# Filter taps summed in four strips of the array with moving powers and then transposed; VectorE takes the norms' constants; products in two halves

## The chip, the cores and the metric

The kernel runs on one core of a Trainium2 chip. The metric is the device time of one execution in microseconds, and the median of several runs counts. TensorE multiplies matrices into PSUM, VectorE and ScalarE work elementwise on SBUF and PSUM, GpSimd works elementwise on SBUF alone, and SyncE issues the transfers.

## What is computed

The input is 16 batches of 256 tokens with 128 channels. Four residual layers follow each other, each on a layer norm of its input; everything before the first expert layer is the part that this case is about.

```python
x = L0_attn_a_u
x = x + _L0_attn_a_ref(_layernorm(x, axis=-1), ...)   # long convolution
x = x + _L0_ffn_ref(_layernorm(x, axis=-1), ...)      # 8 experts, the best 2 of each token
x = x + _L0_attn_b_ref(_layernorm(x, axis=-1), ...)   # causal attention, 16 heads, 4 query sets
x = x + _L0_ffn_ref(_layernorm(x, axis=-1), ...)

# in _L0_attn_a_ref: the filter K, and its product with the input in the frequency domain
at = dt[:, None, None] * A[None, None, :] * t[None, :, None]
K = jnp.einsum('mn,mln->ml', C_re, jnp.exp(at))
y = jnp.fft.irfft(u_f * k_f, n=2 * L_)[..., :L_]
return y.transpose(0, 2, 1) + u * D
```

## The kernel before

Each engine has a queue written out by hand; what stands in it runs in that order, and engines wait for each other by semaphores. The program has five stages: the taps of the filter, the convolution, the first experts, attention, the second experts. In the profile the taps and the convolution take the first 81 us.

**Taps.** The filter K of 256 taps for 128 channels is a sum over 64 states of decaying powers. `z` holds the decay rates. `grid` (L508) multiplies `z` by the tap numbers 0 to 63, ScalarE makes `powers` of it with Exp (L490), in five pieces of 8, 8, 16, 16 and 16 columns of `z` (`GRIDS`); VectorE makes four of the grids and GpSimd the fourth. `leap` holds the four leaps of 64 taps, and `weight` (L527) is leap times `C_re`. TensorE (L551) takes 32 groups of four channels: `powers` (128 columns) is the weight that is loaded, `weight` (16 columns) the operand that moves, and each group writes 128 x 16 values into bank 6. When all 32 are done (`tapped`), VectorE (L537) and ScalarE (L494) move halves of the bank into `ktap`, VectorE adds the skip weight `skip_d` to tap 0 (L542), and TensorE transforms `ktap` with `taps` (L561). ScalarE copies the result to `khat` (L498).

**Convolution.** The 16 batches go through in four chunks of four batches. For each chunk VectorE takes statistics (L384, L388), GpSimd adds epsilon to the variance (`vareps`, L361) and raises it to -1/2 (`rstd`, L363), and for chunks 1 to 3 it also makes `neg_mean` (L395) and `offset` (L398). ScalarE normalizes the chunk with them (L414); of chunk 0 VectorE does that itself (L404). Then the two halves of the sequence are folded (L420): VectorE takes the differences, GpSimd the sums, and both of chunk 0 are VectorE's. TensorE transforms the folded chunk into banks 0 to 3 (L620), VectorE multiplies these banks by `khat` in eight products (L631), GpSimd combines the products in four steps into `yhat` (L642, L644), TensorE transforms back in 16 matrix instructions (L654), and VectorE adds the result to `stream` (L662). TensorE's queue has the forward transform of chunk ch + 1 ahead of the inverse of chunk ch. GpSimd also cuts the low halves of the expert weights (L602) in between, from what ScalarE has scaled and rounded (L575, L577).

**Later stages.** Every later norm goes the same way in groups of four tiles: VectorE L352 and L356, GpSimd L361 and L363, VectorE L369. There are 24 of them: 8 each ahead of the first experts, attention and the second experts. In the expert stages VectorE also subtracts halves (L873) and accumulates (L916), GpSimd subtracts the other halves (L880), and TensorE works at L850 and L904.

## Time and profile before

| What | Value |
|---|---|
| Median of 3 runs | 842.37 us (841.85 to 843.05) |
| The profiled execution | 843.33 us |
| Its span in the trace | 841.6 us |
| TensorE busy in the span | 789.6 us, 94% |
| ScalarE busy | 707.8 us, 84% |
| VectorE busy | 658.0 us, 78% |
| GpSimd busy | 559.9 us, 67% |
| Chain that ended last | TensorE 64%, ScalarE 12%, VectorE 8%, GpSimd 5%, issue 9% |

All times within the trace count from the start of the span. The shares are means over stages with different limits, so a stage is read from its own rows: the chain of work in order of time says which engine each stretch waited for, and the timeline says what stood around it. A matrix product in 32-bit floats shows as two matrix instructions in the trace, a transpose as one.

### The profile page before, as it was taken

What the parts mean: (1) busy time and instruction counts of PE and PEld (TensorE: products, weight loads), DVE (VectorE), ACT (ScalarE), POOL (GpSimd) and SP (SyncE); (2) the same over time, 40 slices, a digit from 0 to 9 for tenths busy, and PEclk for the clock granted to TensorE, in tenths of its full rate; (3) what the DMA queues carried; (4) which work ended last, traced back from release to release, by engine and by line L of the source; (5) the groups of instructions that cost most, each with busy time, mean ns of one, the idle gap of its engine ahead of it and who ended that gap; (6) DMA issues with size and microseconds to landing.
All of it is one profiled execution on the core that took longest, in us unless ns stands there. A gap on an engine that the chain in (4) does not pass through costs nothing.

```text
span 841.6 us, 20311 instructions
## 1 busy us (share of the span) xinstructions
PE 789.6 (94%) x7689; PEld 437.8 (52%) x7689; DVE 658.0 (78%) x1925; ACT 707.8 (84%) x888; POOL 559.9 (67%) x631
## 2 busy tenths in 40 slices
PE   6699998899999899999999999999999999999995
PEld 6344676566677433333333333333333777777774
DVE  5686899999997566777777777777645999888884
ACT  4431897788889799999999999999998899999984
POOL 4694556455543688888888889888887554445442
PEclk9999999999999899999999999999999999999998
DMA  9201000000003323343333434433310000000000
GB/s 291 78 26 76 2 2 2 2 2 1 2 17 87 99 80 95 91 93 92 96 93 82 91 101 102 101 95 87 102 22 1 2 14 14 15 14 14 14 14 16
DMA packets 38521, 46.87 MB, mean 56 GB/s; under 512 B 6185, under 2 KB 23858, under 8 KB 38418
## 3 DMA queue, kind: packets, MB, share of 16 engines
q1 hardware_dynamic: 38418, 45.51, 20.7%
q8 instruction: 62, 1.02, 0.5%
q14 instruction: 41, 0.34, 0.1%
HBM read 28.71 MB, written 16.78 MB: 54 GB/s over the span
## 4 chain that ended last, share of the span: by engine, by line
PE 64%; ACT 12%; issue 9%; DVE 8%; POOL 5%; DMA 0%; ACTq 0%; POOLq 0%
PE psum L904 16%; PE psum L850 16%; PE psum L1202 12%; ACT prob L1160 11%; PE psum L1151 5%; PE psum L1260 4%; PE psum L654 4%; DVE mixed L916 3%; POOL prob L1175 2%; PE psum L551 2%; PE psum L1044 1%; PE psum L725 1%; PE psum L620 1%; DVE hidden_parts_first L873 1%; PE psum L700 1%
## 5 line engine op out<-in xcount | busy, mean ns | idle before, releaser
L1160 ACT ACTIVATE prob<-psum 128x1536 f32<-128x1536 f32 x256 | 347.8, 1498 | 17.4 <-PE psum L1151 17.4
L1202 PE MATMUL psum<-prob,vstack 128*32 128x256 f32 (+1 forms) x2048 | 207.3, 500 | 1.6 <-DVE o_tok L1210 1.6
L850 PE MATMUL psum<-xt_parts,w_parts 128*128 128x512 f16 x768 | 186.7, 379 | 2.7 <-POOL wqkv_parts L602 2.7
L916 DVE SCALAR_TENSOR_TENSOR mixed<-psum,comb_y,mixed 128x128 f32<-128x128 f32 x512 | 143.1, 339 | 2.1 <-PE psum L904 2.1
L880 POOL TENSOR_TENSOR hidden_parts_second<-hidden_second,hidden_parts_second 128x512 f16<-128x512 f32 x64 | 78.9, 1234 | 91.7 <-ACT hidden_parts_second L866 91.7
L880 POOL TENSOR_TENSOR hidden_parts_first<-hidden_first,hidden_parts_first 128x512 f16<-128x512 f32 x64 | 77.9, 1221 | 77.2 <-ACT hidden_parts_first L866 77.1
L864 ACT ACTIVATE hidden_first<-psum,b 128x512 f32<-128x512 f32 x128 | 88.4, 690 | 31.0 <-PE psum L850 23.9
L1170 POOL TENSOR_SCALAR_AFFINE_SELECT prob<-prob 128x512 f32<-128x512 f32 x128 | 82.5, 644 | 42.1 <-ACT prob L1160 36.5
L1151 PE MATMUL psum<-qstack,kstack 32*128 32x512 f16 x768 | 100.4, 387 | 9.1 <-POOL prob L1175 4.4
L1151 PEld LDWEIGHTS psum<-qstack,kstack 32*128 32x128 f16 x768 | 24.9, 91 | 159.0 <-ACT prob L1160 137.3
L850 PEld LDWEIGHTS psum<-xt_parts,w_parts 128*128 128x128 f16 x768 | 71.9, 99 | 67.2 <-POOL wqkv_parts L602 2.8
L864 ACT ACTIVATE hidden_second<-psum,b 128x512 f32<-128x512 f32 x128 | 88.3, 690 | 19.2 <-PE psum L850 15.5
L904 PE MATMUL psum<-w_parts,hidden_parts_first 128*128 128x128 f16 x1536 | 96.0, 219 | 8.3 <-issue 5.2
L904 PEld LDWEIGHTS psum<-w_parts,hidden_parts_first 128*128 128x128 f16 x1536 | 90.3, 98 | 25.1 <-issue 13.3
L904 PEld LDWEIGHTS psum<-w_parts,hidden_parts_second 128*128 128x128 f16 x1536 | 90.9, 98 | 16.4 <-issue 2.0
L904 PE MATMUL psum<-w_parts,hidden_parts_second 128*128 128x128 f16 x1536 | 96.0, 219 | 1.4 <-DVE mixed L916 1.0
L1210 DVE STREAM_TRANSPOSE o_tok<-psum 128x512 f32<-128x512 f32 x64 | 45.9, 717 | 56.8 <-PE psum L1202 56.7
L866 ACT ACTIVATE hidden_parts_first<-psum,b 128x512 f16<-128x512 f32 x128 | 88.4, 691 | 0.0
L866 ACT ACTIVATE hidden_parts_second<-psum,b 128x512 f16<-128x512 f32 x128 | 88.3, 690 | 0.0
L1175 POOL TENSOR_SCALAR_AFFINE_SELECT prob<-prob 128x1280 f32<-128x1280 f32 x64 | 85.1, 1330 | 4.6
L1172 POOL TENSOR_SCALAR_AFFINE_SELECT prob<-prob 128x512 f32<-128x512 f32 x128 | 82.5, 645 | 0.0
L1202 PEld LDWEIGHTS psum<-prob,vstack 128*32 128x32 f32 x2048 | 47.3, 109 | 53.7 <-issue 30.9
(133 smaller groups left out, 1050.8 us busy)
## 6 DMA issues: line engine op xcount, KB each, us to landing
qstack<-qk_parts SPq DMA_DIRECT2D x128, 128.0 KB, 3.5
qk_parts<-parts SPq DMA_DIRECT2D x64, 192.0 KB, 3.2
kstack<-qk_parts SPq DMA_DIRECT2D x128, 32.0 KB, 3.4
stream<-L_attn_a_u SPq DMA_DIRECT2D x4, 512.0 KB, 8.0
kept_x<-stream SPq DMA_DIRECT2D x4, 512.0 KB, 2.7
out<-mixed SPq DMA_DIRECT2D x8, 256.0 KB, 2.3
mirror<-u_mirror SPq DMA_DIRECT2D x4, 256.0 KB, 7.1
w_whole<-L_ffn_W SPq DMA_DIRECT2D x1, 1024.0 KB, 9.4
```

The lines of the kernel that those rows point to most:

```text
L850: last = e.matmul(bank(u % 4), m.w1[:, w_part, ex, cols], xt_parts[:, s, x_part, :], start=(n == 0), stop=(n == len(PRODUCTS) - 1))
L864: last = e.activation(m.hidden[:, r, k, :], bank(u % 4), ACT.Relu, scale=scale, bias=bias)
L866: last = e.activation(m.hidden_parts[:, r, 0, k, :], bank(u % 4), ACT.Relu, scale=scale, bias=bias)
L880: e.tensor_tensor(m.hidden_parts[:, r, 1, 1, :], m.hidden[:, r, 1, :], m.hidden_parts[:, r, 0, 1, :], ALU.subtract).then_inc(low_second, 1)
L904: last = e.matmul(to[:, t * P:(t + 1) * P], h_[:, t * P:(t + 1) * P], w_, start=(n == 0), stop=(n == len(terms) - 1))
L916: last = e.scalar_tensor_tensor(out=m.y[:, t0 + t, :], in0=bank(down_bank(m, i))[:, t * P:(t + 1) * P], scalar=comb_y[:, s, t, ex:ex + 1], ...
L1151: last = e.matmul(to[:, i * BANK:(i + 1) * BANK], kstack[at, s, c, keys * P:(keys + 1) * P], queries, start=True, stop=True)
L1160: e.activation(prob[:, n % PROBS, :], psum[:, TILE * (n % 2):TILE * (n % 2 + 1)], ACT.Exp, scale=SCALE)\
L1170: e.affine_select(blocks[:, 0:3:2], blocks[:, 0:3:2], [[0, 2], [0, 2], [1, P]], ALU.is_ge, 0.0, base=0, channel_multiplier=-1)
L1172: e.affine_select(blocks[:, 4:6], blocks[:, 4:6], [[0, 2], [0, 2], [1, P]], ALU.is_ge, 0.0, base=0, channel_multiplier=-1).then_inc(masked, 1)
L1175: e.affine_select(blocks[:, 0:5], blocks[:, 0:5], [[0, 5], [0, 2], [1, P]], ALU.is_ge, 0.0, base=0, channel_multiplier=-1).then_inc(masked, 1)
L1202: last = e.matmul(to[SLOT * lane:SLOT * (lane + 1)], vstack[:, b % 2, keys, first:first + SLOT], weights_of(n - t, lane, keys, pair), star ...
```

## The change

The taps are computed with the operands exchanged. The group's `weight`, padded with zeros to 32 columns, is loaded, and its `powers` (128 columns) move. Group g writes 32 partitions of PSUM, in strip g % 4, so four groups in a row lie in four different strips of the array, and 32 groups fill banks 6 and 7. The result lies across: ScalarE copies bank 6 after group 15 and VectorE copies bank 7 after group 31 into `tap_rows`, TensorE transposes eight blocks into banks 4 and 5, and the moves to `ktap` read from there. `grid` is now VectorE's alone, and the weights stand before the second grid. The transfers of `eye` and `skip_d` are issued before `forward`.

For the norms VectorE adds epsilon itself, right behind its aggregates, in all 28 places, and makes `offset` of chunks 1 to 3 with one instruction (`neg_mean` is gone). The fold's difference and the next `offset` stand between the two halves of a chunk's products. ScalarE cuts the first expert weights after the moves to `ktap`, and GpSimd's cuts stand elsewhere in its queue.

```diff
     def scalar_taps(e):
...
         for i, (lo, hi) in enumerate(GRIDS):
-            if i == GPSIMD_GRID:
-                e.wait_ge(gridded_too, 1)
-            else:
-                e.wait_ge(gridded, i + (i < GPSIMD_GRID))
+            if i + 1 == len(GRIDS):
+                e.wait_ge(tapped, 1)
+                e.copy(tap_rows[:, 0:LANES, :].rearrange("p g l -> p (g l)"), bank(6)).then_inc(rows_first, 1)
+            e.wait_ge(gridded, i + 1)
...
-        scalar_cut(e, 0, w1_flat, w1_flat, s_w1, 16)
-        e.wait_ge(tapped, 1)
+        e.wait_ge(taps_turned, 2)
         for r in range(2):
             last = e.copy(*ktap_move(1, r))
         last.then_inc(ktap_copied, 1)
+        scalar_cut(e, 0, w1_flat, w1_flat, s_w1, 16)
...
+        e.wait_ge(tapped, 2)
+        e.tensor_copy(tap_rows[:, LANES:, :].rearrange("p g l -> p (g l)"), bank(7)).then_inc(rows_second, 1)
         vector_conv_first(e)
-        e.wait_ge(tapped, 1)
+        e.wait_ge(taps_turned, 2)
...
-            last = e.matmul(bank(6)[:, 16 * g:16 * (g + 1)], powers[:, 2 * g:2 * (g + 1), :].rearrange("p s l -> p (s l)"),
-                            weight[:, 2 * g:2 * (g + 1)].rearrange("p s j q -> p (s j q)"), start=True, stop=True)
-        last.then_inc(tapped, 1)
+            lane, at = g % LANES, g // LANES * 2 * QUARTER
+            last = e.matmul(psum[SLOT * lane:SLOT * (lane + 1), 6 * BANK + at:6 * BANK + at + 2 * QUARTER],
+                            weight[:, g].rearrange("p z s j q -> p (z s j q)"),
+                            powers[:, 2 * g:2 * (g + 1), :].rearrange("p s l -> p (s l)"), start=True, stop=True)
+            if g % (GROUPS // 2) == GROUPS // 2 - 1:
+                last.then_inc(tapped, 1)
+        e.wait_ge(s_small, SMALL)
+        for half, landed in enumerate((rows_first, rows_second)):
+            e.wait_ge(landed, 1)
+            for n in range(LANES * half, LANES * (half + 1)):
+                last = e.transpose(psum[:, 4 * BANK + n * P:4 * BANK + (n + 1) * P], tap_rows[:, n, :], eye[:])
+            last.then_inc(taps_turned, 1)
...
+    def vector_conv_offset(e, ch):
+        tiles = slice(ch * CONV_TILES, (ch + 1) * CONV_TILES)
+        e.wait_ge(conv_norm.rstd, ch + 1)
+        e.scalar_tensor_tensor(out=offset[:, tiles], in0=meanvar[:, tiles, 0], scalar=-1.0, in1=rstd[:, tiles],
+                               op0=ALU.mult, op1=ALU.mult).then_inc(offset_ready, 1)
...
     def vector_conv(e):
         vector_conv_stats(e, 2)
-        vector_fold(e, 1)
+        vector_conv_offset(e, 1)
         e.wait_ge(khat_copied, 2)
         for ch in range(CONV_CHUNKS):
-            vector_products(e, ch)
+            vector_products(e, ch, 0)
+            if ch + 1 < CONV_CHUNKS:
+                vector_fold(e, ch + 1)
             if ch + 2 < CONV_CHUNKS:
-                vector_fold(e, ch + 2)
+                vector_conv_offset(e, ch + 2)
+            vector_products(e, ch, 1)
```

How the queues change is told best at three places. The first is VectorE's queue from the aggregates of chunk 0 (L388 before, L393 now) to the skip weight; of the eight norms the first two are shown. Before:

```order
L388 BN_AGGR meanvar<-stats 128x2 x8
L508 TENSOR_TENSOR powers<-z,tap_in 128x1024
L404 TENSOR_SCALAR normed<-stream,meanvar,rstd 128x128
L404 TENSOR_SCALAR normed<-mirror,meanvar,rstd 128x128
...
L420 TENSOR_TENSOR folded<-normed 128x512 x2
L537 COPY ktap<-psum 64x2x2x32 x2
L542 TENSOR_TENSOR ktap<-ktap,skip_d 1x128
```

And in the changed kernel, at the same place of the same engine:

```order
L393 BN_AGGR meanvar<-stats 128x2 x8
L364 TENSOR_SCALAR vareps<-meanvar 128x8
L515 TENSOR_TENSOR powers<-z,tap_in 128x1024 x2
L540 COPY tap_rows<-psum 128x512
L410 TENSOR_SCALAR normed<-stream,meanvar,rstd 128x128
L410 TENSOR_SCALAR normed<-mirror,meanvar,rstd 128x128
...
L426 TENSOR_TENSOR folded<-normed 128x512 x2
L544 COPY ktap<-psum 64x2x2x32 x2
L549 TENSOR_TENSOR ktap<-ktap,skip_d 1x128
```

The epsilon, GpSimd's grid and the copy of bank 7 have come in, and the norms of chunk 0 now stand behind the copy, which waits for the last group of taps. The second place is GpSimd's queue from the cuts of the first expert weights (`w1_parts`) to the first combines of chunk 0. Before:

```order
L602 TENSOR_TENSOR w1_parts<-w1_whole,w1_parts 128x512
L420 TENSOR_TENSOR folded<-normed 128x512
L361 TENSOR_SCALAR vareps<-meanvar 128x8
L363 TENSOR_TENSOR rstd<-vareps,minus_half 128x8
L395 TENSOR_SCALAR neg_mean<-meanvar 128x8
L398 TENSOR_TENSOR offset<-neg_mean,rstd 128x8
L602 TENSOR_TENSOR w1_parts<-w1_whole,w1_parts 128x512
L642 TENSOR_TENSOR yhat<-prod 128x512
L644 TENSOR_TENSOR yhat<-prod 128x512
```

And in the changed kernel:

```order
L618 TENSOR_TENSOR w1_parts<-w1_whole,w1_parts 128x512 x3
L426 TENSOR_TENSOR folded<-normed 128x512
L368 TENSOR_TENSOR rstd<-vareps,minus_half 128x8
L657 TENSOR_TENSOR yhat<-prod 128x512
L659 TENSOR_TENSOR yhat<-prod 128x512
```

Four instructions between the fold of chunk 1 and the first combine have left: three went to VectorE, and the cut went ahead of the fold. The third place is VectorE's queue at the products of chunk 0. Before:

```order
L388 BN_AGGR meanvar<-stats 128x2 x8
L420 TENSOR_TENSOR folded<-normed 128x512
L631 TENSOR_TENSOR prod<-psum,khat 128x512 x8
L420 TENSOR_TENSOR folded<-normed 128x512
L384 BN_STATS stats<-stream 128x6
```

And in the changed kernel:

```order
L393 BN_AGGR meanvar<-stats 128x2 x8
L364 TENSOR_SCALAR vareps<-meanvar 128x8
L403 SCALAR_TENSOR_TENSOR offset<-meanvar,rstd 128x8
L646 TENSOR_TENSOR prod<-psum,khat 128x512 x4
L426 TENSOR_TENSOR folded<-normed 128x512
L403 SCALAR_TENSOR_TENSOR offset<-meanvar,rstd 128x8
L646 TENSOR_TENSOR prod<-psum,khat 128x512 x4
L389 BN_STATS stats<-stream 128x6
```

The fold of chunk 1 stands behind four products now, and the `offset` of chunk 2, which waits for GpSimd's `rstd` of that chunk, stands before the other four.

## Rows read from the trace of the kernel before

**Rows 1.** The chain in order of time, first 81 us: start, length, engine, output, line

```profile
21.63 3.60 PE psum L620 x4
25.23 2.75 PE psum L561 x16
28.01 0.75 ACT khat L498 x2
28.76 3.08 ACT normed L414 x8
31.91 1.77 POOL folded L420
...
34.09 1.68 POOL rstd L363
...
37.45 1.27 POOL yhat L642
...
41.63 1.23 POOL yhat L644
...
43.00 8.80 PE psum L654 x16
...
73.63 6.98 PE psum L654 x16
```

**Rows 2.** Line L551: weight loads, shortest, median and longest in ns

```profile
L551 PEld LDWEIGHTS psum<-weight,powers x64: 288/334/334, 7.8 to 21.2; 128*128 128x128 f32 x64
```

**Rows 3.** Timeline around 92 us: start, length, engine, line, instruction

```profile
92.18 0.97 PEld L725 LDWEIGHTS psum<-wg,xt 128*128 128x128 f32 x8
```

**Rows 4.** Stretches of 1 us: five engines' busy time, granted clock, DMA share, GB/s

```profile
34.00:35.00 1.00, 0.50 (x1) 0.50 (x2) 1.00 (x3) 0.00 (x0) 0.92 (x2) 0.50 0.00 0
45.00:46.00 1.00, 1.00 (x2) 0.34 (x1) 1.00 (x3) 0.00 (x0) 0.83 (x3) 0.50 0.00 0
```

**Rows 5.** Timeline from 3 to 14 us, VectorE and ScalarE

```profile
3.63 3.00 DVE L508 TENSOR_TENSOR powers<-z,tap_in 128x512 f32<-128x512 f32 x2
...
6.55 1.19 DVE L527 TENSOR_TENSOR weight<-leap,tap_in 64x256 f32<-64x256 f32 x2
...
7.78 1.23 DVE L508 TENSOR_TENSOR powers<-z,tap_in 128x1024 f32<-128x1024 f32 x1
...
11.15 1.20 DVE L508 TENSOR_TENSOR powers<-z,tap_in 128x1024 f32<-128x1024 f32 x1
...
12.38 1.06 ACT L490 ACTIVATE powers<-powers 128x1024 f32<-128x1024 f32 x1 [1.34 <-DVE powers L508]
```

**Rows 6.** Timeline: matrix instructions in four strips in attention, and a set of transposes

```profile
402.69 1.07 PE L1202 MATMUL psum<-prob,vstack 128*32 128x256 f32 x16
...
65.37 0.60 PE L700 MATMUL psum<-eye,normed 128*128 128x128 f32 x4
```

**Rows 7.** Timeline of VectorE: first norm of chunk 0, folds, skip weight, aggregates, PSUM reads

```profile
14.24 0.35 DVE L404 TENSOR_SCALAR normed<-stream,meanvar,rstd 128x128 f32<-128x128 f32 x1 [1.89 <-POOL rstd L363]
...
16.41 1.29 DVE L420 TENSOR_TENSOR folded<-normed 128x512 f32<-128x512 f32 x2
...
22.34 0.28 DVE L542 TENSOR_TENSOR ktap<-ktap,skip_d 1x128 f32<-1x128 f32 x1
...
26.41 0.64 DVE L388 BATCH_NORM_AGGREGATE meanvar<-stats 128x2 f32<-128x6 f32 x8
...
52.06 1.27 DVE L662 TENSOR_TENSOR stream<-psum,stream 128x512 f32<-128x512 f32 x2
```

**Rows 8.** Shares by line of the chain between 81 and 165 us

```profile
by line: DVE mixed L916 17.7%; PE psum L850 11.8%; PE psum L904 11.4%; issue 11.3%; DVE hidden_parts_first L873 8.9%; DVE normed L369 7.5%; POOL hidden_parts_first L880 4.0%; DVE stats L352 3.9%; POOL wqkv_parts L602 2.8%; PE psum L725 2.0%
```

**Rows 9.** GpSimd's groups of the same stretch: busy us and mean ns

```profile
L361 POOL TENSOR_SCALAR vareps<-meanvar 128x4 f32<-128x4 f32 x6 | 2.1, 342 | 6.9 <-DVE meanvar L356 6.9
```

**Rows 10.** A small VectorE instruction by its line: shortest, median, longest ns

```profile
L783 DVE TENSOR_SCALAR comb_y<-comb x16: 169/174/1169, 82.8 to 800.1; 128x32 f32<-128x32 f32 x16
```

More of the change, by code:

```diff
@@ L189, in build_in @@
         mirror = sb("mirror", [P, BATCH, D], of=own)
-        offset, neg_mean = sb("offset", [P, TILES], of=own), sb("neg_mean", [P, TILES], of=own)
+        offset = sb("offset", [P, TILES], of=own)
         folded = sb("folded", [P, 2, 2, BANK], of=own)
@@ L200, in build_in @@
         powers = sb("powers", [P, 2 * GROUPS, QUARTER], of=own)
-        weight = sb("weight", [P, 2 * GROUPS, 2, QUARTERS], of=own)
+        weight = sb("weight", [P, GROUPS, 2, 2, 2, QUARTERS], of=own)
+        tap_rows = sb("tap_rows", [P, GROUPS // LANES, 2 * QUARTER], of=own)
         ktap = sb("ktap", [P, HALVES, D], of=own)
@@ L513, in gpsimd_taps @@
         e.memset(weight[:], 0.0).then_inc(weight_zeroed, 1)
-        e.wait_ge(z_ready, 1)
-        grid(e, GPSIMD_GRID).then_inc(gridded_too, 1)
     def vector_taps(e):
@@ L521, in vector_taps @@
         grid(e, 0).then_inc(gridded, 1)
-        grid(e, 1).then_inc(gridded, 1)
         e.wait_ge(leaped, 1)
@@ L1321, in gpsimd_conv @@
         gpsimd_low_weights(e, 0, 0)
-        gpsimd_low_weights(e, 0, 1)
         gpsimd_conv_rstd(e, 1)
-        gpsimd_low_weights(e, 0, 2)
+        for n in range(1, CONV_CHUNKS):
+            gpsimd_low_weights(e, 0, n)
         gpsimd_fold(e, 1)
         gpsimd_conv_rstd(e, 2)
-        gpsimd_low_weights(e, 0, 3)
         for ch in range(CONV_CHUNKS):
```

62 lines of the change are left out of this document (30 added, 32 removed).

## The prediction

> **What bounds the kernel now.** I read the chain of work in order of time first, since shares of busy time average over five stages. [rows 1] show the first 81 us as one chain: the taps on TensorE until 21.63, the first forward transforms (3.60) and the taps' own transform until 28.01, the copy of khat, ScalarE's norm of chunk 1, GpSimd's fold, its rstd and its four combines until 42.86, and from 43.00 TensorE alone, back to back, until 80.61. So two things set the end of this part: when TensorE can begin its unbroken run at 43.0, and how fast that run goes. The later stages follow whatever comes out of it. In 81 to 165 us the chain is mostly VectorE's [rows 8]; behind that it is TensorE's, and ScalarE's in attention, which the shares of the whole chain in the table bear out.
>
> Then I read the pace. The 64 loads of L551 stand in 13.8 us, one per 0.216 us (7.8 to 21.63, [rows 1, 2]), while eight loads of the same shape at L725 take 0.97, one per 0.12 [rows 3]. So the taps ran at about half pace, though the granted clock shows 1.00 there. The clock's rows show the lower level (0.50, that is 1.2 GHz) at 34 and at 45 us [rows 4]. The inverse of chunk 0 takes 8.80 and that of chunk 3 takes 6.98 for the same 16 instructions [rows 1]: 1.8 us are the clock's, after TensorE had stood idle ahead of 43.0.
>
> **Grids and powers: nothing.** VectorE's queue up to the last grid ends at 11.15 + 1.20 = 12.35 [rows 5]. After: start at 3.63, a grid of 512 at half of 1.23 (0.62), the weights 1.19, a grid of 512 (0.62), one of 1024 (1.23), statistics and aggregates as between 7.78 + 1.23 and 11.15 (2.14), the epsilon 0.2, two grids of 1.2: 12.85 at most, less the overlap of neighbours, some 12.5. GpSimd's grid had held VectorE up (the first two grids took 3.00 instead of 1.24), and that pays for the one VectorE takes over. ScalarE's last Exp (12.38, 1.06) gets the copy of bank 6 ahead of it, at most 0.75 as the two khat copies took together [rows 1]; I take 0.5, so the last powers stand at 14.0.
>
> **The sum over the taps: 13.83 becomes a tail of about 1.** TensorE now starts at about 5.6 and keeps up with the powers, so only the last eight groups count, 16 instructions of 128 columns. No row shows this form. The nearest is L1202, four strips, 16 instructions of 256 columns in 1.07 at full pace [rows 6]; 128 columns at half pace are as much. The bounds are 0.5 (full pace) and 16 x 0.216 = 3.5 (no overlap between strips). I take 1.1, as the form with four strips is the near one: done at 15.1. The Trainium skill (TensorE: Matmul & The Clock Gate, what matters for your kernels) gives small-M packing with three strips 2.38 times the speed, not 3; at that efficiency the tail would be 1.4 and every later number 0.3 more. The packed row here agrees better with full overlap.
>
> **Copy, transposes, norm: on VectorE's path.** The copy of bank 7 is a PSUM read of 128x512, half of the 1.27 of two [rows 7]: 15.75. Four transposes take 0.60 at full pace [rows 6], so eight take at most 2.4 at half pace, done by 17.5. VectorE meanwhile does the eight norms of chunk 0 (14.24 to 16.41: 2.17) and two folds (1.29) [rows 7]; it cannot start them earlier, since the copy is ahead of them in its queue. The first forward transform starts after the first fold: 15.75 + 2.17 + 0.65 = 18.6, instead of 21.63: **3.0 earlier**. The moves to ktap and the skip weight took 21.63 to 22.62; they now end at 19.2 + 1.0 = 20.2, and hide under the two forward transforms (3.60, until 22.2). The transposes hide under the norms; were that cover gone, they would cost 1.8.
>
> From the first forward to khat the work is the same: 28.01 - 21.63 = 6.38 before. It is bound by the pace: all ten products of the taps at half pace would add 20 x 0.216 - 2.75 = 1.6, and all at full pace (20 x 0.12) would save up to 0.9 with the rest of the forwards. I take the same 6.4: khat at 25.0. VectorE's second statistics end at 27.05 now [rows 7]; they move with the skip weight (2.4 earlier) and carry two epsilons of 0.2, so offset stands at 25.3, just ahead of the end of ScalarE's khat copies at 25.75. The scaling of the expert weights fits between ScalarE's moves and the khat copies. The norm of chunk 1 then ends at 28.9 instead of 31.84.
>
> **GpSimd between the fold and TensorE's run: 2.4.** Before: fold to 33.68, epsilon until 34.09, rstd to 35.77, then neg_mean, offset and a cut until 37.45, four combines until 42.86, that is 5.4 for 4 x 1.23 because VectorE's fold of chunk 2 stood between them [rows 1]. After: fold, rstd, four combines. Removed: 0.41 - 0.08, 1.68 - 0.1, and 0.5. The last combine ends at 28.9 + 1.85 + 1.75 + 0.1 + 4.9 = 37.5. The added wait is VectorE's: offset of chunk 2 waits for rstd at 32.5, and the second four products (2.4) are queued behind it, until 35.0. GpSimd's third combine needs them at 35.0, so it just holds. Before, they had all been there at 37.3.
>
> **TensorE's run: 1.8.** The forwards of chunk 1 need the fold at 30.7 (two, at half pace, until 34.2) and the late products (two more, until 36). So TensorE is idle for about 1.5 ahead of the inverse instead of the 3.4 before, and I take the fall to half pace at 45 us as gone. Bounds: 0 and 1.8. Then the run needs its inputs: combines of chunk 1 have to end by 47.9 and come, by the same count on GpSimd (fold, rstd, cut, four combines behind 37.5, with one clash), at 47; products of chunk 3 have a margin near 1. So the run stays unbroken, but barely.
>
> **The 24 later epsilons: +1.2.** GpSimd's six in 81 to 165 us took 0.34 each [rows 9] and were mostly off the path. On VectorE each is a wait for the aggregates and a small instruction, 0.17 by the shortest L783 [rows 10], 0.2 with its wait. Six of them in the stretch that VectorE leads [rows 8] cost 1.2. The bounds are below nothing (rstd comes 0.3 earlier to norms that TensorE waits for) and 6 x 1.17, the longest L783. The other 18 lie in stages led by other engines: nothing.
>
> **Sum.** 3.0 + 2.4 + 1.8 - 1.2 = 6.0. The profiled execution took 843.33 (span 841.6 and 1.7 around it), 1.0 above the median; against the median 842.37 the forecast is **836.3**.
>
> **Rivals.** (a) Better, 834.2: the clock comes up ahead of the taps' transform (-0.9) and the epsilons hide (-1.2). For it: 16 instructions of the taps' transform took 2.75 before, where half pace makes 3.5 [rows 1], so the clock came up within it. (b) The clock falls again ahead of the inverse of chunk 0: 838.1. For it: TensorE is idle from 27 to 30.7 and runs in pieces afterwards. (c) GpSimd becomes the bound of the run: its margin of 0.9 at the combines of chunk 1 is gone, each later chunk waits 0.6, some 2 in all: 838.3. For it: it is busy without a gap from 28.9 to 47. (d) The change doesn't do what it says, strips do not overlap: TensorE needs 13.8 from 5.6, ends at 19.4, VectorE's copy and norms start only then, 4.3 later than forecast, so the first term turns into -1.3 and 840.6 results. Against it: [rows 6].
>
> (e) Slower: VectorE's epsilons meet GpSimd's halves. L783, the same operation on a small SBUF tile, took 0.17 mostly and 1.17 once, as long as a GpSimd instruction [rows 10]. If eleven of the 24 stall that long on the path, 12.9 is lost against a gain of 7.2: 848.1. It decides from the seventh on. Against it: the median of L783 is 0.174 [rows 10], and it stands in the same stages. The GPSIMD Engine Reference of the Trainium skill (Specifications) says that GpSimd shares its SBUF interfaces with VectorE instructions in a two-port mode or with two SBUF inputs. By that rule every epsilon is open to it; the 1.169 of one row agrees that it happens.
>
> **Chances and range.** About 0.2% (1.7 us) is what a measurement of this kernel can tell from no change. Forecast 0.43, (a) 0.14, (b) 0.14, (c) 0.12, (d) 0.06, two or more of the losses together (840 to 843) 0.05, (e) 0.06. Faster: the first four and most of (d), 0.88. Same: 0.06. Slower: (e), 0.06. The range takes in (a) to (d), with the tail's bound on the low side: 833.3 to 840.9; outside lie (e), part of the combined losses and little below.
>
> **What would show it.** In the changed profile: 64 instructions of L559 ending near 15; the first forward (L636) at 18.6; khat (L504) at 25; the first combine (L657) at 32.6 and the first inverse (L669) at 37.5, taking 7.0 with a granted clock of 1.00; TensorE unbroken to about 73.4, where before it was 80.6; L364 at 0.15 to 0.2 in the later stages, with few near 1.1. Wrong if the copy of bank 7 ends after 17, if the second four products start after 34, or if TensorE waits for L659 within its run.

## The result, and the profile after

The changed kernel takes 836.43 us (median of 4 runs, 835.31 to 837.43). The kernel before took 842.11 beside it (4 runs, 841.85 to 843.05). The ratio is 0.993, with a 95% interval of 0.9913 to 0.9947: 5.7 us faster, and all of the interval lies beyond 0.2%. The forecast was 836.3. The profiled execution took 837.43, the longest of the four, with a span of 835.7 against 841.6 before.

The page of the changed kernel, its first part: busy time, share of the span and instructions of each engine.

```profile
span 835.7 us, 20324 instructions
PE 781.6 (94%) x7697; PEld 426.4 (51%) x7697; DVE 656.1 (79%) x1958; ACT 709.0 (85%) x889; POOL 550.6 (66%) x596
```

TensorE is busy 8.0 us less and GpSimd 9.3 less. VectorE is as busy as it was (656.1 against 658.0), though it now has 28 epsilons more. None of this says where the time went. For that I read the chain in order of time, as in [rows 1]. Its columns are start, length, engine, output, line.

```profile
24.97 0.17 DVE offset L403
...
25.16 3.19 ACT normed L420 x8
...
28.42 1.77 POOL folded L426
30.19 1.62 POOL rstd L368
31.83 1.22 DVE offset L403
33.05 1.81 DVE prod L646 x3
...
34.90 3.78 PE psum L636 x4
38.69 7.05 PE psum L669 x16
...
67.57 6.98 PE psum L669 x16
```

Against [rows 1] the norm of chunk 1 starts 3.6 us earlier, TensorE's run starts at 38.69 instead of 43.00 and the first inverse takes 7.05 instead of 8.80. The run ends at 67.57 + 6.98 = 74.55, where it ended at 80.61: 6.06 earlier, and the whole span is 5.9 shorter. All of the gain thus lies in the first 75 us. But the way to TensorE's run is not the one I had described: VectorE stands in it twice (`offset` 1.22, products 1.81), and then two forward transforms that take 3.78. GpSimd's combines are not in it.

The timeline shows what stood around these places. Its columns are start, length, engine, line, operation, output and inputs, and in brackets how long the engine was idle and what released it.

```profile
13.47 1.08 PE L559 MATMUL psum<-powers,weight 128*32 128x128 f32 x16 [0.35 <-ACT powers L496]
...
14.62 0.69 DVE L540 COPY tap_rows<-psum 128x512 f32<-128x512 f32 x1 [2.58 <-PE psum L559]
...
18.23 3.75 PE L636 MATMUL psum<-folded,forward 128*128 128x512 f32 x4 [1.75 <-DVE folded L426]
...
23.81 0.75 ACT L504 COPY khat<-psum 128x512 f32<-128x512 f32 x2 [2.89 <-PE psum L577]
24.44 0.61 DVE L364 TENSOR_SCALAR vareps<-meanvar 128x8 f32<-128x8 f32 x1
...
31.77 1.26 POOL L657 TENSOR_TENSOR yhat<-prod 128x512 f32<-128x512 f32 x1
31.83 1.22 DVE L403 SCALAR_TENSOR_TENSOR offset<-meanvar,rstd 128x8 f32<-128x8 f32 x1 [2.76 <-POOL rstd L368]
...
35.55 1.28 POOL L659 TENSOR_TENSOR yhat<-prod 128x512 f32<-128x512 f32 x1
```

The last 16 instructions of the taps take 1.08, the copy of bank 7 begins at 14.62 after an idle time of 2.58, and the first forward transform starts at 18.23. `offset` of chunk 2 has eight elements per partition and takes 1.22: it starts 0.06 after GpSimd's combine and ends with it. GpSimd's fourth combine ends at 35.55 + 1.28 = 36.83, and TensorE is then still in its forward transforms until 38.68.

Stretches of the same trace: length, busy time of five engines, granted clock, DMA share, GB/s.

```profile
27.00:30.00 3.00, 0.00 (x0) 0.00 (x0) 1.21 (x2) 1.34 (x4) 1.84 (x2) 0.78 0.34 117
30.00:34.00 4.00, 3.71 (x4) 1.17 (x4) 2.17 (x3) 0.92 (x3) 4.00 (x4) 0.50 0.00 0
...
38.00:42.00 4.00, 4.00 (x9) 1.67 (x8) 4.00 (x7) 3.55 (x4) 3.64 (x4) 0.88 0.00 0
```

TensorE is idle from 27 to 30, as it had been from 30 to 34 before. The clock is at its lower level (0.50, 1.2 GHz) from 28.7 to 38.9, that is until just after the inverse has begun.

### The profile page after: what moved, and what is told of

Same layout as the page of the kernel before. It is cut to its first block, busy times and chain, and to the rows that moved or that the text cites. A ratio compares the mean times of both kernels' runs of the same rounds, so it can differ in the third digit from the quotient of the medians.

```text
span 835.7 us, 20324 instructions
## 1 busy us (share of the span) xinstructions
PE 781.6 (94%) x7697; PEld 426.4 (51%) x7697; DVE 656.1 (79%) x1958; ACT 709.0 (85%) x889; POOL 550.6 (66%) x596
## 4 chain that ended last, share of the span: by engine, by line
PE 57%; DVE 14%; ACT 12%; issue 9%; POOL 6%; ACTq 0%; DVEq 0%
PE psum L919 14%; PE psum L865 13%; PE psum L1217 12%; ACT prob L1175 10%; PE psum L1166 5%; DVE mixed L931 5%; PE psum L1275 4%; PE psum L669 3%; POOL prob L1190 2%; DVE hidden_parts_first L888 2%; PE psum L1059 1%; PE psum L740 1%; PE psum L636 1%; DVE normed L374 1%; POOL prob L1187 1%
## 5 line engine op out<-in xcount | busy, mean ns | idle before, releaser
L895 POOL TENSOR_TENSOR hidden_parts_second<-hidden_second,hidden_parts_second 128x512 f16<-128x512 f32 x64 | 77.2, 1207 | 94.5 <-ACT hidden_parts_second L881 94.5
L1185 POOL TENSOR_SCALAR_AFFINE_SELECT prob<-prob 128x512 f32<-128x512 f32 x128 | 84.2, 658 | 44.9 <-ACT prob L1175 39.5
L1225 DVE STREAM_TRANSPOSE o_tok<-psum 128x512 f32<-128x512 f32 x64 | 45.9, 717 | 54.0 <-PE psum L1217 54.0
L1187 POOL TENSOR_SCALAR_AFFINE_SELECT prob<-prob 128x512 f32<-128x512 f32 x128 | 82.9, 648 | 0.0
## 6 DMA issues: line engine op xcount, KB each, us to landing
qk_parts<-parts SPq DMA_DIRECT2D x64, 192.0 KB, 3.2
```

The source lines that it names most:

```text
L895: e.tensor_tensor(m.hidden_parts[:, r, 1, 1, :], m.hidden[:, r, 1, :], m.hidden_parts[:, r, 0, 1, :], ALU.subtract).then_inc(low_second, 1)
L1185: e.affine_select(blocks[:, 0:3:2], blocks[:, 0:3:2], [[0, 2], [0, 2], [1, P]], ALU.is_ge, 0.0, base=0, channel_multiplier=-1)
L1187: e.affine_select(blocks[:, 4:6], blocks[:, 4:6], [[0, 2], [0, 2], [1, P]], ALU.is_ge, 0.0, base=0, channel_multiplier=-1).then_inc(masked, 1)
```

## Theories

My theory at this point: the gain is made by two nearly independent parts, the taps (khat and the first forward earlier) and the norms with the halves (GpSimd's way shorter). TensorE's start is held by `offset` of chunk 2 ahead of the second products, and by the clock. The later epsilons cost about nothing in sum. The rivals: the clock alone decides the start (then a TensorE kept at work would begin earlier); the taps gain nothing by strips (then another order of strips changes nothing or much); the later epsilons cost time that the first 75 us hide. The kernels ran in three groups, each on one chip: e1 to e4 beside a median of 842.10 for the kernel before, e5 to e8 beside 841.94, e9 to e12 beside 842.04. Across these groups I compare ratios and stages of the traces.

## Experiments

**e1: the changed kernel again.**

> The changed kernel once more, as the yardstick for the three kernels beside it on the same chip. Both theories expect what it gave: 5.7 us less than before (ratio 0.993), TensorE's unbroken run from 38.7 to 74.6 us, and VectorE's offset of chunk 2 stretched to about 1.2 us.

Measured: 836.71 (5 runs, 835.33 to 837.43), ratio 0.9937 [0.9924, 0.9951]. The profiled execution was the shortest of these, 835.33 with a span of 833.6. Its chain at the start of TensorE's run:

```profile
34.82 1.98 PE psum L636 x4
...
36.90 7.11 PE psum L669 x16
```

Same program, same order, and 1.8 us earlier at the start of the run than in the other trace (38.69), since the same four instructions take 1.98 instead of 3.78. In this trace the clock had fallen earlier (0.94 granted in 22 to 27, 0.50 in 27 to 30) and had come back by 34 (1.00 in 34 to 38). The runs of the changed kernel spread over 2.1 us, and at this place 1.8 of them lie between the two traces. It is not the only place: e8 has a trace that starts early and ends late.

**e2: the taps alone.** Norms, products and GpSimd's order as in the kernel before; the taps in four strips.

```diff
-        vector_norm_eps(e, norm, i, t0, n)
-    def vector_norm_eps(e, norm, i, t0, n):
+    def gpsimd_norm_rstd(e, norm, i, t0, n):
...
-            vector_products(e, ch, 0)
-            if ch + 1 < CONV_CHUNKS:
-                vector_fold(e, ch + 1)
+            vector_products(e, ch)
             if ch + 2 < CONV_CHUNKS:
-                vector_conv_offset(e, ch + 2)
-            vector_products(e, ch, 1)
+                vector_fold(e, ch + 2)
```

> Only the taps' part of the change (operands exchanged, four strips, transposes, the grids, the order of the transfers, ScalarE's cut behind the moves); the norms' constants and the products as before. Theory: the parts add up. khat stands 4 us earlier than before, GpSimd still has its epsilon, neg_mean, offset and a cut ahead of the combines, so TensorE's run starts near 40, 2.7 to 3.5 us earlier than before, and the time is 837.5 to 839.5. Rival: the gain is the queue's order behind khat, and without it the earlier khat is waited away: 841 or more.

Measured: 839.86 (11 runs, 838.20 to 840.63), ratio 0.9973 [0.9964, 0.9982]. The chain of its profiled execution:

```profile
38.42 1.23 POOL yhat L656
...
39.79 8.71 PE psum L666 x16
```

The start is 3.2 earlier than before and set by GpSimd, as it was before. The inverse keeps its long form (8.71 against 8.80), with 0.70 granted in 38 to 42.

**e3: the norms and the halves alone.** The taps as in the kernel before, the rest as changed.

```diff
-            last = e.matmul(psum[SLOT * lane:SLOT * (lane + 1), 6 * BANK + at:6 * BANK + at + 2 * QUARTER],
-                            weight[:, g].rearrange("p z s j q -> p (z s j q)"),
-                            powers[:, 2 * g:2 * (g + 1), :].rearrange("p s l -> p (s l)"), start=True, stop=True)
+            last = e.matmul(bank(6)[:, 16 * g:16 * (g + 1)], powers[:, 2 * g:2 * (g + 1), :].rearrange("p s l -> p (s l)"),
+                            weight[:, 2 * g:2 * (g + 1)].rearrange("p s j q -> p (s j q)"), start=True, stop=True)
```

> Only the other part (epsilon and offset on VectorE, fold and offset between the halves of the products, GpSimd's new order); the taps as before. Theory: GpSimd's way from the fold to the fourth combine is 2.4 us shorter, the inverse of chunk 0 starts near 40.5 and ends 2.4 to 4.2 us earlier, time 838 to 840. Rival: without the earlier khat the forwards of chunk 1 at half pace set the start, and less than 1.5 us is left: 840.6 or more.

Measured: 838.61 (5 runs, 838.06 to 840.16), ratio 0.9961 [0.9947, 0.9975]. The chain of its profiled execution:

```profile
35.25 1.22 DVE offset L401
...
38.32 1.98 PE psum L624 x4
...
40.40 7.11 PE psum L657 x16
```

The parts add up. The taps alone bring 842.10 - 839.86 = 2.2, the norms and halves 3.5, together 5.7, and both at once 5.4 in the same comparison. The end of the last inverse in the traces says the same: 80.61 before, 77.3 in e2 (3.3 earlier), 76.3 in e3 (4.3), 72.8 in e1 (7.8). The gain of the long first inverse, 1.7, belongs to the norms and the halves: e3 has it and e2 doesn't. And `offset` with its 1.22 is in e3's chain too.

**e4: `offset` of the next chunk but one behind the second four products.**

```diff
+            vector_products(e, ch, 1)
             if ch + 2 < CONV_CHUNKS:
                 vector_conv_offset(e, ch + 2)
-            vector_products(e, ch, 1)
```

> The changed kernel with the offset of the next-but-one chunk behind the second four products instead of ahead of them. The same numbers are computed. Theory: the second products waited for GpSimd's rstd and then for GpSimd's combine, from 29.1 to 33.0 us, and the forwards of chunk 1 behind them were what TensorE's run started from. Now they start at 29.1, the last two forwards follow the first two at once (34.1 at the latest), and the run starts when the fourth combine is done, near 36.8 instead of 38.7: 1.5 to 2 us less than the changed kernel beside it, about 834.5. Rival: GpSimd sets the start anyway and ScalarE's norm of chunk 2 comes later, so the run breaks further on: no gain, or a loss up to 1 us.

Measured: 836.61 (5 runs, 835.25 to 838.46), ratio 0.9937 [0.9924, 0.9951], the ratio of e1. The timeline where the run starts:

```profile
30.35 5.47 PE L636 MATMUL psum<-folded,forward 128*128 128x512 f32 x8 [6.14 <-DVE prod L646]
36.92 5.39 PE L669 MATMUL psum<-yhat,inverse 128*128 128x512 f32 x12 [1.09 <-POOL yhat L659]
```

The wait that I had blamed was gone, the eight forwards ran in one piece and were done by 35.8, and the inverse started at 36.92, as in e1 to 0.02. Now GpSimd's fourth combine sets it. Two ways are level there (in e1 the forwards end at 36.80 and GpSimd's fourth combine at 36.75), so taking one away gives nothing; it only moves who is waited for. That the stall at `offset` costs time was thus refuted for a changed kernel whose run starts early; no trace shows this order with the late start.

**e5: TensorE kept at work in its gap.** Five unused products (ten instructions, into bank 7, which is free by then) follow the last forward of chunk 0; nothing is left out.

```diff
             tensor_forward(e, 0, pos)
+        e.wait_ge(khat_copied, 2)
+        for n in range(WARM):
+            e.matmul(bank(7), forward[:, 0:P], taps[:, 0, 0:BANK], start=True, stop=True)
```

> The changed kernel with five more matrix products on TensorE (forward by 512 columns of taps into bank 7, whose content nobody reads before it is written anew) where it stands idle from about 26 to 30 us, behind the last forward of chunk 0. They compute nothing that is used. Theory: the spread of the changed kernel (835.3 to 837.4) is the clock's: in the idle gap TensorE falls to 1.2 GHz, and whether it is back by 34 or by 38.5 us decides whether the last two forwards of chunk 1 take 2 or 3.8 us. With the gap filled they always take under 2, the granted clock shows 1.00 from 27 to 40 us, TensorE's run starts at 36.9 at the latest, and the median falls to about 835.5 with a spread below 1.5. Rival: the spread comes from later stages; then the median stays within 0.5 of the changed kernel and the spread too.

Measured: 836.07 (5 runs, 835.60 to 836.24), ratio 0.9932 [0.9915, 0.9948]. The timeline and a stretch:

```profile
25.69 4.45 PE L585 MATMUL psum<-taps,forward 128*128 128x512 f32 x10
30.16 1.96 PE L640 MATMUL psum<-folded,forward 128*128 128x512 f32 x4
```

```profile
30.00:34.00 4.00, 2.10 (x5) 0.68 (x4) 2.30 (x3) 1.05 (x3) 4.00 (x4) 1.00 0.00 0
```

The clock stayed at 1.00 (2.4 GHz) from 27 us to the end of the run, and the two pairs of forwards of chunk 1 took 1.96 and 1.98. Yet the run started at 36.85, against 36.90 in e1: at full clock the start waits for VectorE's products and for GpSimd. These five runs spread over 0.64 us instead of 2.1, so nothing in their times points to the late start at 38.69; only one of them has a trace. So the clock moves the start by up to 1.8 us, but what sets the early start isn't the clock. The ratios of e1 and e5 can't be told apart.

**e6: the 24 later epsilons back on GpSimd.**

```diff
-        vector_norm_eps(e, norm, i, t0, n)
...
     def gpsimd_norm_rstd(e, norm, i, t0, n):
+        if norm is not conv_norm:
+            vector_norm_eps(e, norm, i, t0, n)
```

> The changed kernel with the 24 epsilons behind the convolution back on GpSimd, those of the convolution on VectorE. Prediction's term: 1.2 us less than the changed kernel (835.4). Rival, from the trace after: the stretch from the end of TensorE's run to the end took 761.15 us against 761.0 before, so they cost nothing and the time is that of the changed kernel within 0.5.

Measured: 835.37 (6 runs, 833.48 to 837.13), ratio 0.9920 [0.9902, 0.9939]. The ratio is 0.0017 below e1's (1.4 us), and the intervals overlap, so the time alone doesn't settle it. The stages do. `o_tok` (L1225, the first and the last of 64 in attention) cuts the span in stages; the columns are shortest, median and longest ns, and first and last start in us. First the changed kernel, then e6.

```profile
L1225 DVE STREAM_TRANSPOSE o_tok<-psum x64: 716/717/718, 286.8 to 643.5; 128x512 f32<-128x512 f32 x64
```

```profile
L1226 DVE STREAM_TRANSPOSE o_tok<-psum x64: 716/717/718, 286.2 to 643.1; 128x512 f32<-128x512 f32 x64
```

From the last `o_tok` to the end of the span are 835.7 - 643.5 = 192.2 us, and in e6 834.1 - 643.1 = 191.0, as before (841.6 - 650.6 = 191.0). The place of the loss can be pointed at. The chain of the changed kernel near 663 us:

```profile
661.29 0.04 DVE vareps L364
...
663.15 0.97 issue
664.12 1.64 DVE hidden_parts_second L888
```

And of e6 at the same place of the program, where TensorE leads again by 662.5:

```profile
661.36 1.05 DVE mixed L932 x4
...
662.54 1.50 PE psum L920 x24
```

The epsilon itself (in the chain with 0.04) costs nothing to speak of. But it shifts VectorE against GpSimd, and the next small instruction and the next subtraction come to stand beside GpSimd's and take as long as those. Timeline of the changed kernel, VectorE and GpSimd:

```profile
662.90 2.31 POOL L895 TENSOR_TENSOR hidden_parts_second<-hidden_second,hidden_parts_second 128x512 f16<-128x512 f32 x2
```

```profile
663.01 1.18 DVE L1253 SCALAR_TENSOR_TENSOR in_bounds<-rden,in_bounds 128x128 f32<-128x128 f32 x1
664.12 1.64 DVE L888 TENSOR_TENSOR hidden_parts_second<-hidden_second,hidden_parts_second 128x512 f16<-128x512 f32 x1
```

In e6 these two take 0.28 and 0.68. Behind the run, e6 and e8 differ in nothing but these epsilons, and their traces have the clock at its lower level there for nearly the same time (6.8 and 6.9 us). From the end of the run to the end of the span e6 takes 834.1 - 73.4 = 760.7 and e8 takes 835.8 - 73.05 = 762.75: 2.0 less with them on GpSimd.

**e7: every later epsilon twice on VectorE,** to double the suspected cost.

```diff
+        e.wait_ge(norm.agg, i + 1)
+        e.tensor_scalar(vareps[:, t0:t0 + n], meanvar[:, t0:t0 + n, 1], EPS, None, ALU.add).then_inc(norm.first_eps, 1)
+        e.wait_ge(norm.first_eps, i + 1)
         vector_norm_eps(e, norm, i, t0, n)
```

> The changed kernel with each of the 24 later epsilons computed twice on VectorE, one behind the other, each with its wait. If an epsilon there costs its 0.2 us on the path in the six places that VectorE leads, the time rises by 1.2; if all 24 cost it, by 5; if they cost nothing, by less than 0.5.

Measured: 841.91 (12 runs, 839.60 to 842.93), ratio 0.9999 [0.9988, 1.001]. All of the gain is gone. In its trace the span is 839.2, 3.5 more than the changed kernel's, and this is the row of the second epsilon of each pair:

```profile
L362 DVE TENSOR_SCALAR vareps<-meanvar x24: 170/180/1215, 47.9 to 688.4; 128x4 f32<-128x4 f32 x24
```

The median is 0.18, and 24 times 0.18 make 4.3, if all stood on the path. By stages (`o_tok` from 288.3 to 646.8): 2.7 more than in the changed kernel's first trace from the end of TensorE's run to the first `o_tok`, 1.8 more in attention, 0.2 more in the last stage, 4.7 together, against a run that ended 1.2 earlier. But about 1.7 of the 2.7 are the clock's: this trace has it at the lower level for 6.8 us in that stage, the other for 3.4. Against e8, with 6.9, the stage takes 1.3 more. So the ten epsilons that were added in the first stage cost about 0.13 each, the eleven in attention 0.16, and those behind the run together some 3.3. Part of the 5.2 us in the medians isn't in the span at all: the executions of this kernel took 2.5 to 4.5 us more than their spans, all others 1.7 to 2.0. I can't say why; the kernel also has one semaphore more for each kind of norm. Of this run only the spans are evidence; their median is 838.45, where that of the changed kernel's four runs is 834.65.

**e8: the same strips in another order.** From group 8 on, groups come as 0, 4, 1, 5, 2, 6, 3, 7 of each eight, so that two groups of one strip come in a row.

```diff
+            g = step if step < 8 else step // 8 * 8 + step % 2 * LANES + step % 8 // 2
```

> The changed kernel with the groups of the three pieces of eight taken in the order 0, 4, 1, 5, 2, 6, 3, 7, so that both groups of a strip stand next to each other: four matrix instructions in a row go to one strip. The same numbers are computed. Theory: the 16 instructions take 1.08 us because neighbours lie in different strips and overlap; with four in a row in one strip they take 2 or more (four of 0.107 to 0.213 each, strips one after another where they don't overlap), and everything behind is 1 later. Rival: the instructions come one per 0.044 us whatever the strip, as the queue lets them; then they take 1.08 again.

Measured: 836.75 (4 runs, 835.98 to 837.51), ratio 0.9937 [0.9918, 0.9957]. The last 16 instructions:

```profile
13.58 1.10 PE L560 MATMUL psum<-powers,weight 128*32 128x128 f32 x16 [0.32 <-ACT powers L496]
```

1.10 instead of 1.08. That four neighbours lie in four different strips is not what makes the taps fast here: two in a row in one strip are as fast. What is left as its reason is the exchange itself: 32 columns are loaded instead of 128, and an instruction comes every 1.08 / 16 = 0.07 us against 0.216 before [rows 1, 2]. No run takes the strips away altogether, so how much of this is overlap stays open.

This trace says one thing more. Behind the taps the kernel is the changed one, and its run starts early, at 37.14, with full pace in the late forwards (1.98). Yet this execution is the longest of its four (837.51, span 835.8). The time went after the run: 213.65 to the first `o_tok`, where e1 has 211.98. So a late start of the run is not all of the spread.

**e9: both level ways shortened.** GpSimd takes `rstd` of chunk 2 ahead of the fold, and its fourth cut of the first weights goes to the end; VectorE takes `offset` of chunk 2 ahead of the fold and that of chunk 3 behind the products.

```diff
             vector_products(e, ch, 0)
+            if ch == 0:
+                vector_conv_offset(e, 2)
...
-            if ch + 2 < CONV_CHUNKS:
-                vector_conv_offset(e, ch + 2)
             vector_products(e, ch, 1)
+            if ch == 1:
+                vector_conv_offset(e, 3)
...
-        for n in range(1, CONV_CHUNKS):
-            gpsimd_low_weights(e, 0, n)
+        gpsimd_low_weights(e, 0, 1)
+        gpsimd_low_weights(e, 0, 2)
+        gpsimd_conv_rstd(e, 2)
         gpsimd_fold(e, 1)
-        gpsimd_conv_rstd(e, 2)
...
+                gpsimd_low_weights(e, 0, 3)
```

> The changed kernel with GpSimd's rstd of chunk 2 ahead of its fold of chunk 1 instead of behind it, the fourth cut of the first expert weights at the end of its convolution work, VectorE's offset of chunk 2 ahead of the fold, and that of chunk 3 behind the second products. The same numbers are computed. Theory: what sets the earliest start of TensorE's run (36.9 in three kernels) is GpSimd's way fold, rstd, four combines; with rstd gone ahead the fourth combine ends at 35.1 instead of 36.8. Without the filled gap the forwards of chunk 1 at half pace then set the start (30.3 + 2 x 3.4 at worst), so 0 to 1.7 is gained, median 835 to 836.5. Rival: the start is TensorE's own pace alone; nothing is gained.

Measured: 835.14 (6 runs, 834.48 to 835.89), ratio 0.9921 [0.9905, 0.9936]. The ratio is 0.0016 below e1's, with intervals that overlap. The chain:

```profile
28.91 1.21 DVE prod L646 x2
30.14 6.74 PE psum L636 x8
36.88 6.87 PE psum L669 x16
```

Neither VectorE nor GpSimd is waited for behind 30.14. But the clock is at 0.50 in 30 to 34, the eight forwards take 6.74 (8 x 0.84) and the run starts no earlier than in e1. Here the clock is the bound, which it was not in e5.

**e10: e9 and TensorE kept at work** (e5's edit on top of e9).

```diff
+        e.wait_ge(khat_copied, 2)
+        for n in range(WARM):
+            e.matmul(bank(7), forward[:, 0:P], taps[:, 0, 0:BANK], start=True, stop=True)
```

> The kernel before this one, and TensorE's idle gap filled with five products that compute nothing used, as in the kept-busy run. Theory: the forwards run at full pace, TensorE's run starts at 35.2, 1.65 earlier than in the kept-busy run, and the median is 834.4 with a spread below 1. Rival: VectorE or GpSimd run behind in a later chunk, and TensorE's run breaks: no gain over the kept-busy run (836.1).

Measured: 834.58 (6 runs, 833.66 to 836.27), ratio 0.9912 [0.9896, 0.9928]. The timeline:

```profile
31.13 3.60 PE L640 MATMUL psum<-folded,forward 128*128 128x512 f32 x8
35.63 6.67 PE L673 MATMUL psum<-yhat,inverse 128*128 128x512 f32 x15 [0.91 <-POOL yhat L663]
```

Only the two edits together start the run earlier, at 35.63: 1.2 before e1. In this execution the unused products themselves lasted until 31.1 and held the forwards up; at full pace they caught up, and GpSimd set the start again. The span shows nothing of it in this execution, the longest of the six: the stage up to the first `o_tok` took 213.85 against 211.98 in e1, and the span is 834.5 against 833.6. By the medians e10 gains over e9 by 0.0009 in the ratio, well within the intervals. Unlike in e5, the runs still spread over 2.6 us, so that filling the gap makes the runs alike is not shown.

**e11: e10 with the epsilons of the second experts' eight norms on GpSimd.**

```diff
+    def eps_on_gpsimd(norm, i):
+        return norm is expert_norm and i >= FFN_CHUNKS
```

> As the one before, with the epsilons of the eight norms ahead of the second experts back on GpSimd, the others on VectorE. Theory, from the traces: the last stage (from the last transpose of attention to the end) took 191.0 us in the three kernels that have these epsilons on GpSimd and 192.0 to 192.4 in the six that have them on VectorE, while the first experts' stage took 0.7 to 1.2 less with its epsilons on VectorE. So 1.1 less than the run before it, and the last stage is 191.0 again. Rival: the last stage's difference hangs on the phase in which it begins, not on these epsilons; it stays at 192.

Measured: 833.76 (6 runs, 832.61 to 834.92), ratio 0.9902 [0.9885, 0.9919]. The medians differ by 0.8 and the intervals overlap. Its trace:

```profile
L1235 DVE STREAM_TRANSPOSE o_tok<-psum x64: 716/716/718, 285.3 to 642.2; 128x512 f32<-128x512 f32 x64
```

833.0 - 642.2 = 190.8 for the last stage, where e10 had 192.3. Over all traces of this study the rule holds: with these eight epsilons on GpSimd the last stage takes 190.8 to 191.0 (before, e2, e6, e11, e12), with them on VectorE 192.0 to 192.4 (the changed kernel, e1, e3 to e5, e7 to e10). So they cost 1.0 to 1.6 there, although only two of the eight stand in it; the other six stand in attention, which takes 356.7 to 356.9 either way. The clock is not the reason: in all these traces 1.00 is granted from 645 to 825.

**e12: e11, and VectorE's norms of chunk 0 ahead of the copy of bank 7,** with GpSimd's `rstd` of chunks 1 and 2 ahead of its cuts.

```diff
+        vector_conv_first_norm(e)
         e.wait_ge(tapped, 2)
         e.tensor_copy(tap_rows[:, LANES:, :].rearrange("p g l -> p (g l)"), bank(7)).then_inc(rows_second, 1)
-        vector_conv_first(e)
+        vector_conv_first_fold(e)
...
-        gpsimd_low_weights(e, 0, 0)
         gpsimd_conv_rstd(e, 1)
+        gpsimd_low_weights(e, 0, 0)
+        gpsimd_conv_rstd(e, 2)
...
-        gpsimd_conv_rstd(e, 2)
```

> As the one before, with VectorE's eight norms of chunk 0 ahead of the copy of bank 7 and GpSimd's rstd of chunks 1 and 2 ahead of the cuts. Theory: VectorE waits from 12.0 to 14.6 for the last taps with the norms queued behind; with the norms in that gap the first forward starts near 16.2 instead of 18.2, khat at 21.8 instead of 23.8, and TensorE's run near 33.2 instead of 35.2: 2 us less. Rival: ScalarE's cut of the first expert weights (until 20.9) or GpSimd's order holds the offset of chunk 1, and less than 1 is gained.

Measured: 832.84 (5 runs, 830.90 to 833.22), ratio 0.9887 [0.9868, 0.9905]: the fastest kernel of the study, 9.2 us below the kernel before. Its interval lies below that of e1 as a whole (0.9924 to 0.9951), so it beats the changed kernel too, by 0.0050 in the ratios, some 4.2 us. The timeline:

```profile
16.30 2.93 PE L649 MATMUL psum<-folded,forward 128*128 128x512 f32 x4
21.05 0.75 ACT L513 COPY khat<-psum 128x512 f32<-128x512 f32 x2
33.49 7.10 PE L682 MATMUL psum<-yhat,inverse 128*128 128x512 f32 x16 [1.29 <-POOL yhat L672]
```

The norms used the 2.58 in which VectorE had waited for the last taps, the first forward came 1.9 earlier, and the run starts at 33.49, 3.4 before e1. Against e11 the run ends 2.1 earlier (69.41 against 71.49) and the span is 1.9 shorter; the medians differ by 0.9, with intervals that overlap.

## Why the prediction was right

**The chain up to the first forward: right, each number within 0.6.** The tail of the taps took 1.08 (forecast 1.1) and was done at 14.55 (15.1), the copy of bank 7 ended at 15.31 (15.75), the first forward started at 18.23 (18.6). That all came early has a plain reason: the terms for VectorE's grids add up to 12.03, not to the 12.85 that I wrote, and 12.03 is when its last grid ended. The reason given for the tail, overlap of four strips, is not borne out in that form: e8 changes the order within the strips and nothing follows. The number came from [rows 6], and it held, but that is luck as far as the reason goes. The Trainium skill (TensorE: Matmul & The Clock Gate, Why this matters for your kernels) gives 2.38 for three strips, and the estimate of 1.4 for the tail that I had made from it did not come; since the order of strips changed nothing, the 1.08 says little about how well strips overlap.

**khat: earlier than said, and no longer on the path.** It came at 23.81 (forecast 25.0) in one trace and at 22.04 in e1, where the pace had risen before the first forward, as rival (a) had it. That brought nothing. The norm of chunk 1 starts when VectorE's `offset` is there, 24.97 and 24.90 (forecast 25.3), since VectorE has two sets of statistics to do first. My sum gave 3.0 to this term, from the start of the first forward. It was 3.4 there, and 28.42 against 31.91 at GpSimd's fold: 3.5.

**GpSimd's way: right.** From the fold to the end of the fourth combine it took 28.42 to 36.83, 8.4 us, and 8.6 were forecast; before it was 31.91 to 42.86, so 2.5 were gained where the sum had 2.4.

**The added wait: price missed, consequence half seen.** I had named `offset` of chunk 2 as the wait ahead of the second products, and put their start at 32.5. It was 33.05. `rstd` was there at 31.8, 0.7 earlier than counted, but `offset` then took 1.22 beside GpSimd's combine instead of 0.15. That was rival (e)'s mechanism at a place where I hadn't looked for it. e4 shows what it costs at full clock: nothing.

**TensorE's run: the 1.8 came, and another 1.8 could go.** The first inverse took 7.05 (forecast 7.0), and the run was unbroken until 74.55 (73.4). The step that failed is "the start at 37.5". I had taken "two more, until 36" for the late forwards, and they lasted until 38.68 at half pace. Rival (b) had the clock falling, but at the inverse; it fell one step earlier. In e1, at full pace there, the start was 36.90. These 1.8 us are most of the difference between the two traces of this kernel, but e8 shows that an execution can be as long with an early start.

**The later epsilons: +1.2 forecast, +0.15 in the two traces, and 1.5 to 2.2 once the clock is taken out.** From the end of the run to the end of the span are 761.0 before and 761.15 after. Attention is the same (356.8 before, 356.7 now), the last stage takes 1.2 more, and the stage from the end of the run to the first `o_tok` takes 212.25 instead of 213.2. That last gain is not the epsilons' but the clock's. The same 20 us before, in the changed kernel and in e8 (length, five engines' busy time, granted clock, DMA share, GB/s):

```profile
275.00:295.00 20.00, 17.38 (x173) 8.56 (x170) 10.28 (x33) 15.91 (x16) 12.87 (x17) 0.83 0.35 90
275.00:295.00 20.00, 17.34 (x167) 6.01 (x168) 12.10 (x32) 18.67 (x14) 15.81 (x21) 0.91 0.24 53
275.00:295.00 20.00, 17.37 (x146) 4.84 (x145) 10.96 (x29) 17.63 (x13) 15.73 (x21) 0.83 0.23 43
```

A mean of 0.83 over 20 us stands for 6.8 us at 0.50. Read in stretches of 5 us, TensorE has its lower level in this stage for 6.8 us before, for 3.4 in the changed kernel and for 6.9 in e8. All traces fall into these two kinds. With 3.4 us the stage takes 211.9 to 212.3 (the changed kernel, e1, e3 to e5, e9, all with its epsilons on VectorE). With 6.8 or 6.9 it takes 212.8 to 213.5 with them on GpSimd (before, e2, e6) and 213.65 to 213.9 with them on VectorE (e8, e10 to e12). So the second 3.4 us at half the clock cost about 1.7, and at the same clock the ten epsilons of this stage cost 0.15 to 1.1. The step that put a loss where VectorE leads [rows 8] is thus borne out in its direction; before and after could not show it. The 1.2 of the last stage is settled by e6 and e11, and "the other 18 lie in stages led by other engines: nothing" was wrong: the chain of the last stage runs over VectorE around 663 us. Behind the run together, the traces with 6.8 or 6.9 us take 760.7 to 761.3 with all 24 on GpSimd (before, e2, e6) and 762.75 and 762.95 with all on VectorE (e8, e10). Why the clock falls a second time in some executions stays open.

**The sum.** Forecast 3.0 + 2.4 + 1.8 - 1.2 = 6.0. Measured in the two traces: 6.06 earlier at the end of the run, less 0.15, that is 5.9. Two deviations of about 1.1 cancelled: the run started 1.2 late, and the later stages lost 0.15 instead of 1.2. The second was luck, since the epsilons cost more than forecast there and the clock gave it back. In e1's trace, with the clock up, they didn't: 7.8 at the end of the run and 8.0 in the span. The median of the runs lies between these two, and the forecast is nearer to it than its steps deserve. Rival (c), GpSimd as the bound within the run, did not occur: TensorE never waited for L659 behind its start. Rival (d) did not either. Rival (e) was right about the mechanism and wrong by a factor about its weight, and the epsilons were not the ones that stalled: the longest of the 28 took 0.61. Others did, `offset` with 1.22 and `in_bounds` with 1.18 instead of 0.28, and the last stage lost 1.2.

## What to carry to other kernels

Where two engines feed a third in step, removing the wait that the chain shows can gain nothing (e4, e5); look up the second latest before, and shorten both (e10, e12). Before a stage of one trace is set against the same stage of another, compare how long each had the lower clock; here that was worth 1.7 us and hid the cost of the epsilons. An operation of 0.2 us that is moved to another engine is priced by what it then stands beside, so read its place in every stage and not only in the one in which that engine leads. And an engine that waits for a late input, as VectorE did for the last taps, should do first what needs nothing of it.

## What the runs showed of the hardware

**Small instructions on VectorE can last as long as GpSimd's instruction beside them.** The row of `offset` in the changed kernel (shortest, median, longest ns):

```profile
L403 DVE SCALAR_TENSOR_TENSOR offset<-meanvar,rstd x3: 155/1221/1222, 25.0 to 41.7; 128x8 f32<-128x8 f32 x3
```

The same eight columns took 0.155 once and 1.22 twice. Products that read PSUM kept their 2.47 for four beside the same combines. The GPSIMD Engine Reference of the Trainium skill (Specifications) says that the two engines share their SBUF interfaces, with contention for VectorE's instructions in a 2-port mode or with two SBUF inputs, as `offset` has. The trace agrees and adds the price, nearly the whole of GpSimd's instruction (1.22 beside 1.26). An epsilon took 0.61 beside GpSimd's cut of the weights at 24.44, and 0.17 at 9.60.

**The granted clock of the record isn't always the pace.** The first four forward instructions took 3.75 in the changed kernel's profiled execution and 1.96 in e1, with a granted clock of 1.00 in 18 to 22 us in both.

**One program has several clock histories.** In the first trace of the changed kernel TensorE stood idle for 4.36 us ahead of the forwards of chunk 1 (25.93 to 30.29), and the lower level lasted from 28.7 to 38.9. In e1 it had done the work before the gap faster, stood idle for 6.05 (24.16 to 30.21), and the lower level lasted from 26.4 to 33.3. So the longer gap came with the earlier return, and that is 1.8 us at the start of the run. Between the end of the run and attention, 3.4 or 6.8 us at the lower level part the traces by another 1.7.
